# Layers 3, 4 and 5 of a hybrid network in one pipeline, and the projections of layer 7's first item among the last feed-forward products

## The reference

```
x = x + attn_a(ln(x))        # latent attention, 16 heads
x = x + ffn_fp4(ln(x))       # silu(gate) * up, blockwise 4-bit rounding of both inputs
x = x + forget(ln(x))        # linear attention over the BATCH axis (8 steps), elu+1, forget gate
x = x + ffn_fp4(ln(x))       # same weights as before
x = x + conv(ln(x))          # over the batch axis: y[i] = sum_j taps[i-j] * h[j], times h[i]
x = x + local_pair(ln(x))    # 2 x (windowed attention + gated feed-forward)
x = x + lin_attn(ln(x))      # causal linear attention, 16 heads of 64, gated
x = x + local_pair(ln(x))
```

## Time and profile before

| | |
|---|---|
| median of 3 runs | 2079.46 us (2076.47 to 2080.57) |
| the profiled execution's own time | 2078.81 us |
| its span on the core | 2076.7 us |
| mean granted TensorE clock | 0.912 of full |
| PE busy / PEld / DVE / ACT / POOL | 85% / 68% / 67% / 45% / 22% |

### The profile page before, as it was taken

The page is one execution under the profiler, slowest core; times in us unless marked ns, Lnnn a source line. Parts: engine busy times, 40 slices in busy tenths (PEclk is TensorE's granted clock), DMA queues, the critical chain, the costliest instruction groups (busy, mean ns, idle before and its releaser), DMA issues.

```text
span 2076.7 us, 34010 instructions
## 1 busy us (share of the span) xinstructions
PE 1755.0 (85%) x10875; PEld 1415.7 (68%) x10875; DVE 1393.1 (67%) x3623; ACT 936.7 (45%) x2557; POOL 453.3 (22%) x352
## 2 busy tenths in 40 slices
PE   6999986654467699999989789999987999999997
PEld 5888874422246477777777667787775777777776
DVE  4556579646698677787787655566446777777774
ACT  3444432211121456656656445344404566566654
POOL 2200010000001343343343200000003433433440
PEclk9999987655588899999999999999968999999999
DMA  3000000000100000000000000000000000000000
GB/s 138 0 0 0 0 1 0 0 0 0 50 0 1 1 4 3 3 2 3 3 1 3 3 1 0 0 0 0 0 1 0 4 3 3 2 3 3 1 2 23
DMA packets 15104, 13.76 MB, mean 7 GB/s; under 512 B 11286, under 2 KB 14138, under 8 KB 14650
## 3 DMA queue, kind: packets, MB, share of 16 engines
q1 hardware_dynamic: 15034, 12.88, 1.9%
HBM read 9.74 MB, written 1.05 MB: 5 GB/s over the span
## 4 chain that ended last, share of the span: by engine, by line
PE 39%; issue 31%; DVE 24%; ACT 4%; POOL 2%; DVEq 1%; POOLq 0%; ACTq 0%
PE bank L1530 5%; PE bank L1661 3%; DVE arena_ffn L903 3%; DVE arena_attn L918 3%; PE bank L1562 3%; PE bank L1699 3%; DVE ssq L911 3%; PE bank L1550 3%; PE bank L1648 3%; DVE arena_ffn L899 2%; DVE probT L688 2%; PE bank L1724 2%; PE bank L1703 2%; PE bank L1541 2%; DVE nmaxF L681 2%
## 5 line engine op out<-in xcount | busy, mean ns | idle before, releaser
L534 POOL TENSOR_TENSOR arena_ffn<-arena_ffn 128x1024 f32<-128x1024 f32 x60 | 141.3, 2356 | 503.1 <-DVE arena_ffn L903 503.1
L518 POOL TENSOR_TENSOR rstd<-var,mhalf 128x2 f32<-128x2 f32 x48 | 33.4, 695 | 901.2 <-DVE var L643 901.2
L688 DVE COPY probT<-bank 128x512 f32<-128x512 f32 x288 | 196.9, 684 | 25.6 <-PE bank L1541 25.5
L530 POOL TENSOR_TENSOR inv<-ssq,mhalf 128x16 f32<-128x16 f32 x64 | 186.2, 2910 | 69.7 <-DVE ssq L912 69.4
L1550 PE MATMUL bank<-vF,probT 128*128 128x64 f32 x1536 | 195.9, 271 | 5.8 <-DVE probT L688 4.3
L1550 PEld LDWEIGHTS bank<-vF,probT 128*128 128x128 f32 x1536 | 186.5, 192 | 12.8 <-DVE probT L688 12.5
L681 DVE TENSOR_REDUCE nmaxF<-bank 128x2 f32<-128x384 f32 (+1 forms) x192 | 114.8, 598 | 90.1 <-PE bank L1530 89.7
L1530 PE MATMUL bank<-arena_setup 128*128 128x192 f32 (+1 forms) x1024 | 173.0, 302 | 0.0
L1530 PEld LDWEIGHTS bank<-arena_setup 128*128 128x128 f32 x1024 | 155.8, 193 | 12.5 <-issue 1.1
L1371 ACT ACTIVATE arena_conv<-bank,nmaxF 128x192 f32<-128x192 f32 x256 | 105.4, 419 | 115.9 <-DVE nmaxF L681 112.5
L1253 ACT ACTIVATE prob<-bank,nmax 128x128 f32<-128x128 f32 (+1 forms) x256 | 88.7, 428 | 125.0 <-DVE nmax L681 125.0
(11 more groups left out here) (257 smaller groups left out, 4262.4 us busy)
## 6 DMA issues: line engine op xcount, KB each, us to landing
packF<-in_packF SPq DMA_DIRECT2D x1, 3122.0 KB
arena_history<-in_packG SPq DMA_DIRECT2D x1, 2560.0 KB, 9.1
HS<-XH SPq DMA_DIRECT2D x32, 63.5 KB
X<-in_x_tiled SPq DMA_DIRECT2D x1, 1024.0 KB, 4.9
out_dram<-X SPq DMA_DIRECT2D x8, 128.0 KB, 1.9
arena_setup<-in_const_masks_a SPq DMA_DIRECT2D x1, 512.0 KB, 5.4
arena_setup<-in_const_masks_f SPq DMA_DIRECT2D x1, 512.0 KB
HS<-XH SPq DMA_DIRECT2D x32, 0.2 KB
```

The costliest lines, as they stand in the source:

```text
L530: pool.tensor_tensor(inv[:, t, :, 0], ssq[:, t, :, 0], mhalf[:, 0:16], ALU.pow).then_inc(sems["inv_ready"], 1)
L534: pool.tensor_tensor(t1[:, t], t1[:, t], t2[:, t], ALU.add).then_inc(sems["rope_sum"], 1)
L688: dve.tensor_copy(probT[:, u % 2], bank[4 + u % 2][:]).then_inc(sems["pt_copied"], 1)
```

## The change

**One.** The stages "forget", "q" (as the second feed-forward stage is now called) and "conv" become one written-out pipeline. In iteration k the engines treat forget item k, feed-forward input item k-1 and hidden item k-2, and conv item k-3. The feed-forward stage and the convolution get semaphores of their own (prefixes `q_` and `v_`), their own moments (`stats2`, `mv0`, `hvar`, `hrstd`; `statsV` to `rstdV`), `xqT` beside `xT`, and banks of their own: forget 0, 1, 2 and half of 7; feed-forward half of 4, 5, 6 and half of 7; conv 3 and half of 4. Gate and up of a tile now share one bank: the up product waits until silu has read the gate. `forget_pe` transposes XH itself (no copy by POOL), and issues the bias product ahead of the wait for `xT`. POOL's clearing of `keysZ` moves ahead of this pipeline. The hidden layer's `take_hidden` writes `xqT` in place of `xT`.

**Two.** `lin_first` is gone. Its transpose, 16 projection steps and eight `phi` stand between the last feed-forward products of the pair. ACT loads its function tables accordingly: one `prime(ACT.Gelu)` is added, and in the pipeline of part one a `prime(ACT.Silu)` and a `prime(ACT.Exp, 1)` for each item.

DVE:

```diff
                 if kind == "forget":
-                    for s in range(NB + 1):
-                        if s < NB:
-                            forget_step(v, s)
-                        if s:
-                            forget_end(v, s - 1)
-                            norm_apply(v, s - 1)
+                    vf, vq, vc = vals[n:n + 3]
+                    for k in range(NB + 4):
+                        if k < NB:
+                            forget_step(vf, k)
+                        q_quantise(vq, vf, inside(k - 2), inside(k - 1))
+                        if k < NB:
+                            forget_end(vf, k)
+                        if k == NB + 2:
+                            win_open(vals[n + 3], 0, 0)
+                        if inside(k - 3) is not None:
+                            conv_step(vc, k - 3)
+                        if inside(k - 2) is not None:
+                            q_end(vq, k - 2)
+                        if k < NB:
+                            norm_apply(vf, k)
+                        if inside(k - 3) is not None:
+                            norm_apply(vc, k - 3)
+                        if inside(k - 2) is not None:
+                            norm_apply(vq, k - 2)
+                        if inside(k - 1) is not None:
+                            q_h(vq, k - 1)
+                    win_open(vals[n + 3], 0, 1)
                     continue
```

PE (ACT has the same order: `take_tokens`, `forget_act(k + 1)`, `forget_yT(k)`, `q_hqT(k - 2)`, silu's table, `q_take_xT` and `q_silu` of k - 1, exp's table):

```diff
+                    forget_pe(v, 0, vals[n - 1])
+                    for k in range(NB + 3):
+                        if inside(k - 3) is not None:
+                            conv_taps(vc, k - 3, vq)
+                        if k + 1 < NB:
+                            forget_pe(v, k + 1, vals[n - 1])
+                        if k < NB:
+                            forget_out(v, k)
+                        if inside(k - 2) is not None:
+                            q_out(vq, k - 2, v)
+                        if inside(k - 1) is not None:
+                            q_gates(vq, k - 1)
+                    win_open(vals[n + 3], 0)
```

```diff
+            def q_gates(v, i):
+                pe.wait_ge(v.sem("xq_ready"), v.at("xq_ready", i, 1))
+                for t in range(NT):
+                    ins = pe.transpose(bank[4][:, t * P:(t + 1) * P], xq[:, t * P:(t + 1) * P], ident[:])
+                ins.then_inc(v.sem("xT_psum"), 1)
+                pe.wait_ge(v.sem("xT_ready"), v.at("xT_ready", i, 1))
+                for m, done in enumerate(("gate_ready", "up_ready")):
+                    for t in range(NT):
+                        if m:
+                            pe.wait_ge(v.sem("silu_ready"), v.at("silu_ready", i, t + 1))
+                        pe.matmul(bank[5 + t][:, 0:FI], xqT[:, t * P:(t + 1) * P], wguT[:, m, 0:FI], start=True,
+                                  stop=True).then_inc(v.sem(done), 1)
```

The end of the first pair, DVE and ACT (vl is the linear attention, vm the feed-forward):

```diff
+                    phi(vl, 0, 0)
                     gated(vm, NB - 2, 1)
+                    phi(vl, 0, 1)
+                    mlp_end(vm, NB - 2)
+                    phi(vl, 0, 2)
                     hidden_stats(vm, vals[n + 2], NB - 1)
-                    mlp_end(vm, NB - 2)
+                    phi(vl, 0, 3)
                     hidden_apply(vm, vals[n + 2], NB - 1)
...
+                    take_xT(vl, 0, bank[0])
+                    for m in range(5):
+                        take_step(vl, 0, m)
                     take_hidden(vals[n + 3], NB - 1)
+                    take_step(vl, 0, 5)
+                    prime(ACT.Gelu)
                     gelus(vals[n + 3], NB - 1, 1)
+                    for m in range(6, 16):
+                        take_step(vl, 0, m)
```

More of the change, by code:

```diff
@@ L85 @@
 LAG = 2
-AHEAD = ("forget", "lin")
+AHEAD = ("lin",)
 def attn_unit(u, groups):
@@ L829, in ffn4_h, with q_h, q_quantise, q_end @@
                     dve.tensor_tensor(h[:, t], silu[:, t], bank[2 * t + 1][:, 0:FI], ALU.mult).then_inc(sems["h_ready"], 1)
+            def q_h(v, i):
+                for t in range(NT):
+                    dve.wait_ge(v.sem("up_ready"), v.at("up_ready", i, t + 1))
+                    dve.tensor_tensor(h[:, t], silu[:, t], bank[5 + t][:, 0:FI], ALU.mult).then_inc(v.sem("h_ready"), 1)
+            def q_quantise(v, vin, hi, xi):
+                jobs = ([h_job(v, hi)] if hi is not None else []) + ([x_job(v, xi, vin)] if xi is not None else [])
+                if not jobs:
+                    return
+                ch = Chain(dve, v, "quant_chain", 0, q_quantise.links)
+                last = quantise(jobs, ch.mark, ch.wait)
+                q_quantise.links = ch.n
+                if xi is not None:
+                    last.pop().then_inc(v.sem("xq_ready"), 1)
+                if hi is not None:
+                    last.pop().then_inc(v.sem("hq_ready"), 1)
+            q_quantise.links = 0
+            def q_end(v, i):
+                ch = Chain(dve, v, "dve_chain", i)
+                residual(v, i, ch, bank[7][:, 0:T])
+                ch.close()
             def ffn4_end(v, i):
@@ L1451, in _ @@
                 if kind == "forget":
-                    for s in range(NB + 1):
-                        if s < NB:
-                            forget_act(v, s)
-                        if s:
-                            forget_yT(v, s - 1)
-                if kind == "conv":
-                    for i in range(NB):
-                        take_tokens(v, i)
-                    if opens(n):
-                        win_open(vals[n + 1])
+                    vq, vc = vals[n + 1:n + 3]
+                    forget_act(v, 0)
+                    for k in range(NB + 3):
+                        if inside(k - 3) is not None:
+                            take_tokens(vc, k - 3)
+                        if k + 1 < NB:
+                            forget_act(v, k + 1)
+                        if k < NB:
+                            forget_yT(v, k)
+                        if inside(k - 2) is not None:
+                            q_hqT(vq, k - 2)
+                        if inside(k - 1) is not None:
+                            prime(ACT.Silu)
+                            q_take_xT(vq, k - 1)
+                            q_silu(vq, k - 1)
+                            prime(ACT.Exp, 1)
+                    win_open(vals[n + 3])
                 if begins(n):
@@ L1902, in _ @@
                 v = vals[n]
-                if kind.startswith("mlp") or kind == "win" and not begins(n):
+                if kind.startswith("mlp") or kind in ("q", "conv") or kind == "win" and not begins(n):
                     continue
```

297 lines of the change are left out of this document (185 added, 112 removed).

## The result

Before 2080.0 us (median of four runs, 2076.5 to 2084.7), after 2006.8 (2006.2 to 2009.3): ratio 0.965, 95% interval 0.963 to 0.967. (In the later measurements the kernel before had medians of 2075.8 to 2077.0, so part of the 73 us between these two medians is the spread of the kernel before; single executions of it lie between 2075.0 and 2084.7.) The profiled execution of the changed kernel has a time of 2009.3 and a span of 2007.5, 69.2 less than the span before.

The account below looks back on a forecast made before the run. It took layers 3 to 5 to be bound by chains across engines, with neither DVE nor PE full. 2078.8 - 41.0 (pipeline) - 9.0 (pair's end) = 2028.8, median 2029 us; own range 2020 to 2040, wider range 2010 to 2054.

Parts of the forecast that it names:

- the sum: Whole kernel: profiled 2078.8 us less 41.0 (layers 3 to 5 with the opening) and 9.0 (pair's end) gives 2028.8.
- PE warms up: Rival, layers 3 to 5 and pair's end: closely packed PE work raises the clock, 22 us fewer, 2007 us; chance 0.18.
- Iteration by iteration: Pipeline of layers 3 to 5: DVE's remaining waits in iterations 0 to 10 and layer 6's opening, 39.2 us in all.
- opening: Layer 6's opening, behind the pipeline: one DVE wait for POOL stays, 0.8 us; the opening ends at 651.7.
- the dense work: Pipeline of layers 3 to 5: DVE's work from 402.8 on, 209.7 us without waits, ending at 612.5.
- small gaps: Pauses between dependent DVE operations in the pipeline; with them 206.9 us of busy time was taken as 209.7.
- POOL's clearing of `keysZ`: Ahead of the pipeline, at 396 before: costed at nothing as DVE is idle then; 1.8 us if in the way.
- The eight steps behind the last output: Pair's end: layer 7's projection steps 8 to 15 after the last feed-forward output, 0.88 us each, ending at 1211.5.
- PE stays cold: Rival, layers 3 to 5, opening and pair's end: PE stays at half clock, 25 us more, 2054 us; chance 0.20.
- In series: Rival, pipeline of layers 3 to 5: PE's in-order queue lets nothing overlap, 87 us later there, 2157 us; chance 0.05.
- waits that only move: Rival, DVE's waits: some 50 us more than forecast through an overlooked dependency, so no change, 2079 us; chance 0.02.

Follow-up runs that it names:

- before_later: The kernel before, plus five products of 256 columns into a free bank between the 16 projection steps and layer 7's first item; 2070.6 us (ratio 0.996).

## Why the prediction was wrong

**The step that failed is the sum.** "2078.8 - 41.0 - 9.0" takes everything behind layer 7's first scores as it was. The profiled execution lies 19.5 us below 2028.8; 13.9 of them are the last item of layer 7, 3.8 part one, 0.5 part two, the rest the small differences in layer 6 and behind layer 7. In the profile before, that last item stands at 42.9 us although it has no projections, where the full items take 40.3; its PEclk is 0.60. It can be seen in the earlier trace rows, too: the 6 in slice 30 (1505.6 to 1557.5 us) is this item, and my reading of the row, "at or near 2.4 GHz nearly everywhere" but in slices 8 to 14, passed over it, as over the 8 and 7 in slices 6 and 7 and the 8 in slice 31. I had read the clock only in the layers that the change edits. Had I asked there what a start 50 us earlier does, the range would have had to reach 14 us lower, to about 2010 - 14 = 1996. 2007 is the time that my rival "PE warms up" gave, but not its mechanism: it promised 5.1 us less in iterations 1 and 2, and 7.4 in 3 to 7, and the waits there show 0.5 and 1.2. That agreement is chance.

**Part one was right in kind, 3.8 us too small.** 44.8 us came, 41.0 were forecast. Iteration by iteration, forecast and (measured, from the idle times in DVE's timeline): 0: 7.0 (6.8); 1: 3.7 (3.6); 2: 3.9 (3.5); 3 to 7: 7.4 (6.2); 8: 3.4 (3.4); 9: 2.9 (2.7); 10: 10.1 (10.4); opening: 0.8 (0.8). Together 39.2 (37.4), so the waits give 1.8 of the 3.8. Of the other 2.0, 1.8 lie in the start: I let the dense work begin at 402.8, and the second tile's exponentials were there at 401.05. Without the waits DVE needed 209.5 us, where I had taken 209.7; that is luck in part, since 202.4 of them are busy and 7.1 small gaps, and I had put 206.9 and 2.8. POOL's clearing of `keysZ`, which I had put at nothing, ran from 397.14 to 398.95, and beside it DVE's two `norm_apply` operations took 1.79 and 1.60 us in place of 0.39 and 0.34; they end as item 0's first exponentials arrive, so that no more than 0.2 us of it can have reached the chain.

**Part two was right in sum.** 9.5 us for 9.0. My account did not name POOL's early copy, whose wait alone was 3.6 of it. The eight steps behind the last output, which I had at 0.88 us each although gives 7.67 / 8 = 0.96, took 7.3. PE and ACT of the changed kernel, for the earlier trace rows:

```profile
1152.52 1.92 PE L1761 MATMUL bank<-xqT,w1s 128*114 128x256 f32 x6
...
1158.70 1.60 PE L1781 MATMUL bank<-packF,arena_forget 114*128 114x128 f32 x12
1160.14 7.32 PE L1803 MATMUL bank<-arena_history,xT 128*128 128x512 f32 x16
1167.39 0.70 PE L1819 MATMUL bank<-arena_setup 64*128 64x256 f32 x4
```

```profile
1153.25 0.59 ACT L1483 ACTIVATE arena_ffn<-bank 128x512 f32<-128x512 f32 x1
1153.86 1.28 ACT L1353 ACT_TABLE_LOAD   x1
1155.16 0.20 ACT L1353 ACTIVATE primer<-mhalf 128x1 f32<-128x1 f32 x1
1155.27 1.19 ACT L1435 ACTIVATE arena_forget<-bank,b1s 114x256 f32<-114x256 f32 x3
```

Only steps 8 to 15 stand behind the last output. The load starts 0.02 us after the activation ahead of it ends, and the next starts 0.02 after the load. The Trainium skill ("ScalarE: Activation LUTs", What ACT_TABLE_LOAD costs) adds a drain of about 1.38 us per switch; by that part two would have come to 6.2 us, and this trace does not agree.

**The other rivals.** PE stays cold: out, the clock in the pipeline is 0.68 and the gates run at full speed. In series, and waits that only move: out, no `forget_step` behind item 0 waits for ACT.

## What to carry to other kernels

Before summing the parts of a change, go through the stages behind it as well, and ask for each whether its time holds if it starts at another moment; a stage with the same instructions and two durations is the sign. Where TensorE pauses for 1 to 2 us in an otherwise dense loop, a few products into a free bank can cost less than the clock: 15.4 us were gained with them in the kernel before, though none that could be told from noise in the changed one. And compare two versions with such drops taken out of both: 55 us of the 73 are the change's own.

## What was not expected of the hardware

One pause of 1.4 to 1.8 us per 40 us of dense work took the clock to 1.2 GHz in two or three of the seven items behind the first; in most items the same pause did nothing. With 1.5 us of products in the pause, none of 24 items (1 to 6 in four kernels) had a drop. After a drop PE ran at half clock for 6.8 us (items of 43.5), about 10 (items of 45.1), or for 34 us, 30 of them at 99% busy (the last item before). Late in the last item it fell in two kernels with no wait longer than 0.8 us just ahead. The Trainium skill ("TensorE: Matmul & The Clock Gate", HAM oscillation) tells of a kernel whose waits for operands, some 3 to 5 us long, send the array back to half clock in every round. The waits here are shorter, and they did so in some rounds only; which ones changed from kernel to kernel, with differences of 1 to 3 us ahead of layer 7. How much that moves one and the same kernel from run to run differs: eight runs of before_later lie within 3.4 us, those of the kernel before between 2075.0 and 2084.7.
